# A delta-rule phase: convolution one iteration earlier, taps in PSUM, state product on a block-wise u

## The reference, cut to what matters

```python
q = silu(causal_conv4(x @ q_w, conv_q_w)); k = ...; v = ...       # depthwise, 4 taps
beta = sigmoid(x @ b_w)                                           # per token and head
q, k = l2norm(q), l2norm(k); v = v * beta; kb = k * beta
attn = where(strictly_lower, -(kb @ k.T), 0)                      # per chunk, 32 x 32
for i in range(1, 32):                                            # inverse of a unit triangle
    attn[i, :i] += attn[i, :] @ attn[:, :i]
attn = attn + eye; u = attn @ v; w = attn @ kb
for each chunk:                                                   # S is 32 x 32 per head
    u = u - w @ S
    o = q @ S + where(lower, q @ k.T, 0) @ u
    S = S + k.T @ u
o = g * o + (1 - g) * v                                           # g = sigmoid(x @ mix_w + ...)
out = (rms_norm(o) * o_norm_w) @ o_w
```

## Time and profile before

| what | us |
|---|---|
| median of 3 timed runs | 2016.2 (2015.22 to 2023.95) |
| the profiled execution: its span, and no other time of it is recorded | 2017.0 |
| delta phase in that trace, from about 1196 to 1812 | about 616 |
| busy share of the whole span: PE, DVE, ACT, POOL | 62%, 69%, 45%, 55% |

### The profile page before, as it was taken

One profiled execution on the slowest core, in us unless ns is written; L12 is line 12 of the kernel. 1 busy time (PEld: TensorE's weight loads), 2 busy tenths in 40 slices (PEclk: granted clock), 3 DMA queues, 4 the chain that ended last, 5 costly groups with the idle time before them and its releaser, 6 DMA issues. The chain is left out here.

```text
span 2017.0 us, 33672 instructions
## 1 busy us (share of the span) xinstructions
PE 1259.5 (62%) x13844; PEld 595.1 (30%) x13844; DVE 1388.5 (69%) x1689; ACT 915.8 (45%) x1673; POOL 1112.5 (55%) x479
## 2 busy tenths in 40 slices
PE   4464746556474756553488746577767767557875
PEld 1111212121221312120133323244444445443333
DVE  3799999999999999899650023776687668617002
ACT  5555564746556474644232214454455434123220
POOL 1889989899999989999600011322442344412000
PEclk9676768677676777775698877787778777668988
DMA  4827174472808356280299960112312222219997
GB/s 125 198 48 190 45 184 98 102 181 54 206 25 197 84 128 145 54 208 21 93 403 422 421 211 15 43 39 65 76 33 55 65 65 45 65 42 396 405 421 276
DMA packets 193705, 300.04 MB, mean 149 GB/s; under 512 B 82704, under 2 KB 125200, under 8 KB 177168
## 3 DMA queue, kind: packets, MB, share of 16 engines
q1 hardware_dynamic: 188512, 295.17, 48.5%
q10 hardware_dynamic: 4688, 2.19, 0.4%
q0 software_dynamic: 352, 0.52, 0.1%
HBM read 255.37 MB, written 42.47 MB: 148 GB/s over the span
## 5 line engine op out<-in xcount | busy, mean ns | idle before, releaser
L368 POOL TENSOR_TENSOR state<-dx_rep,b_rep 128x2048 f32<-128x2048 f32 x128 | 579.1, 4532 | 66.9 <-PE psum L736 35.7
L736 PE MATMUL psum<-state,sel 128*32 128x512 f32 x1024 | 193.6, 847 | 292.5 <-POOL state L377 292.5
L479 ACT ACTIVATE psum<-delta_rep,a_neg 128x511 f32<-128x511 f32 x512 | 331.5, 684 | 79.8 <-DVE state L598 79.7
L598 DVE TENSOR_TENSOR_SCAN psum<-psum,state 128x1024 f32<-128x1024 f32 x144 | 328.9, 2284 | 33.9 <-POOL state L368 24.0
L598 DVE TENSOR_TENSOR_SCAN state<-psum,state 128x1024 f32<-128x1024 f32 x112 | 255.2, 2279 | 19.9 <-ACT psum L479 19.9
L377 POOL TENSOR_TENSOR state<-state,c_rep 128x1024 f32<-128x1024 f32 x112 | 264.0, 2359 | 0.0
L667 PE MATMUL psum<-xt,w_in 128*128 128x512 f32 x256 | 161.0, 787 | 47.4 <-ACT z_silu L438 26.1
L605 DVE TENSOR_TENSOR state<-psum,c_rep 128x1024 f32<-128x1024 f32 x144 | 176.3, 1224 | 4.9
L736 PEld LDWEIGHTS psum<-state,sel 128*32 128x32 f32 x1024 | 27.5, 128 | 424.4 <-issue 391.4
L476 ACT COPY psum<-zeros 128x2 f32<-128x2 f32 x144 | 23.6, 164 | 257.9 <-DVE state L605 253.2
L1841 PE MATMUL psum<-xt_delta,w_qkv 128*128 128x512 f32 x192 | 111.4, 721 | 12.1 <-DVE attn_t L1655 11.3
(11 more groups left out here) (218 smaller groups left out, 2535.5 us busy)
## 6 DMA issues: line engine op xcount, KB each, us to landing
moe_w_set<-in_w SPq DMA_DIRECT2D x30, 4096.0 KB, 33.1
delta_rep<-delta_scratch SPq DMA_DIRECT2D x128, 256.0 KB, 5.4
dx_rep<-dx_scratch SPq DMA_DIRECT2D x128, 256.0 KB, 8.2
b_rep<-bc_scratch SPq DMA_DIRECT2D x32, 256.0 KB, 4.9
delta_scratch<-delta SPq DMA_DIRECT2D x32, 256.0 KB, 7.8
dx_scratch<-delta_x SPq DMA_DIRECT2D x32, 256.0 KB, 5.8
c_rep<-bc_scratch SPq DMA_DIRECT2D x32, 256.0 KB, 8.0
moe_x<-x_after SPq DMA_DIRECT2D x16, 512.0 KB, 8.5
```

The source lines that it names most:

```text
L368: nc.gpsimd.tensor_tensor(ring[q % RING][:, :, :], dx_rep[u % CHUNKS][:, :, :], free_bcast(b_rep[q // QPB % 2][:, g, :], 1, CB), ALU.mult) ...
L479: ins = nc.scalar.activation(dec[:, i, 1:], delta_rep[u % CHUNKS][:, c, 1:], ACT.Exp, scale=a_neg[:, dt * CB + c, g:g + 1])
L598: nc.vector.tensor_tensor_scan(bx if by_pool(k) else flat, flat, bx, 0.0, ALU.mult, ALU.add).then_inc(S["scan_done"], 1)
L736: ins = nc.tensor.matmul(bank[32 * c:32 * c + 32, :], sel[:, :], ring[q % RING][:, c, :], start=False, stop=(g == NG4 - 1), skip_group_che ...
```

## The change

1. The whole of a unit's convolution (six projects, last taps, taps) stands in its conv iteration, at slots 6 to 12, in two PSUM banks of its own (`cbank`). Last tap and taps work in place in the bank, and the third of VectorE's taps writes `conv_qkv`. A project from the third on waits for VectorE's last tap of the bank (`conv_done`) instead of ScalarE's read.
2. The front starts with silu at slot 0 (q, k) and slot 1 (v); one table set is loaded back, after v. Tokens are turned at slots 1 and 2, statistics at slot 4 (their rows now in 96 partitions), gram at slots 7 and 9, masks at 8 and 10.
3. SP sends x's residual, the next x, the n pair, the t pair, the output store.
4. `u_blk` has 128 partitions by 4 batches by 256 with zeros off its diagonal blocks. ScalarE writes u in four copies, and `k_times_u` is 8 matmuls over all 128 partitions in place of 32 small ones; the state is in one bank.
5. Outputs use one bank (`tbank`): `turn_outputs` at slots 6 and 7, `project_outputs` at 8 and 10, output adds at 9 and 11, each waiting for the one before.
6. POOL takes the carry of the convolution first and its second `solve_below` after the lambda mask. VectorE's solve rows are spread over slots 0 to 5, its products below stand at 6 and 9, and the gates at 7.

```diff
-    u_bank, o_bank, fbank = banks[0], banks[1], banks[6:8]
-    s_bank = lambda p: banks[2 + p]
+    u_bank, o_bank, s_bank, cbank, fbank, tbank = banks[0], banks[1], banks[2], banks[3:5], banks[5:7], banks[7]
...
-                    nc.scalar.copy(xpad[:, t, :, KC - 1:], bank[:, :].rearrange("c (p l) -> c p l", p=NP))
-                    nc.scalar.activation(raw[:, t, :, :], bank[:, :].rearrange("c (p l) -> c p l", p=NP), ACT.Copy,
-                                         scale=conv_w[:, t, KC - 1:KC]).then_inc(S["qkv_read"], 1)
+                    nc.scalar.copy(xpad[:, t, :, KC - 1:], bank)
+                    nc.scalar.activation(bank, bank, ACT.Copy, scale=conv_w[:, t, KC - 1:KC]).then_inc(S["qkv_read"], 1)
...
-                                nc.scalar.activation(u[:, :], u_bank[:, 0:D], ACT.Copy,
-                                                     scale=-1.0 if k % SPG else 1.0).then_inc(S["u_ready"], 1)
+                                for p in range(NP):
+                                    rows = slice(p * C, (p + 1) * C)
+                                    ins = nc.scalar.activation(u_blk[rows, p, :], u_bank[rows, 0:D], ACT.Copy,
+                                                               scale=-1.0 if k % SPG else 1.0)
+                                ins.then_inc(S["u_ready"], 1)
...
-                            nc.vector.scalar_tensor_tensor(raw[:, t, :, :], xpad[:, t, :, k:k + P], conv_w[:, t, k:k + 1],
-                                                           raw[:, t, :, :], ALU.mult, ALU.add).then_inc(
+                            if k == KC - 2 and w:
+                                dve.wait_ge(S["qk_feat"], w)
+                                dve.wait_ge(S["v_feat"], w)
+                            nc.vector.scalar_tensor_tensor(bank if k < KC - 2 else raw[:, t, :, :], xpad[:, t, :, k:k + P],
+                                                           conv_w[:, t, k:k + 1], bank, ALU.mult, ALU.add).then_inc(
...
-                            for p in range(NP):
-                                ins = nc.tensor.matmul(s_bank(p)[g * DK:(g + 1) * DK, hh * DK:(hh + 1) * DK],
-                                                       toks[w % COPIES][batch_rows(p), n, hc], u[batch_rows(p), hc],
-                                                       start=(k % SPG == 0 and hh == 0), stop=True, skip_group_check=True)
+                            ins = nc.tensor.matmul(s_bank[g * DK:(g + 1) * DK, hh * P:(hh + 1) * P],
+                                                   toks[w % COPIES][:, n, hc], u_blk[:, :, hc],
+                                                   start=(k % SPG == 0 and hh == 0), stop=True, skip_group_check=True)
...
-                        pe.wait_ge(S["qkv_read"], NT * w + j - 1)
+                        pe.wait_ge(S["conv_done"], NT * w + j - 1)
...
-                            if m < 5:
-                                project(f, m + 1)
+                            if m in (1, 2):
+                                for n in (0, 1) if m == 1 else (2, 3):
+                                    to_tokens(f, n)
...
+                        if conv is not None and 6 <= m < 6 + NT:
+                            project(a, m - 6)
+                        if front is not None and m in (7, 9):
+                            gram(f, (m - 7) // 2)
```

More of the change, by code:

```diff
@@ L1301, in state_blocks @@
             rows = slice(g * DK, (g + 1) * DK)
[L1302 removed]
+            return (s_bank[rows, 0:KD * P].rearrange("r (h p e) -> r p h e", h=KD, p=NP), state[rows, :, :, rows])
         def iterations(iteration):
@@ L1346, in iteration @@
                                 S[f"t_loaded{solve % 2}"], 16)
-                    if front is not None:
-                        sp.wait_ge(S["n_read"], HS * (front + 1))
+                    if tail is not None:
+                        sp.wait_ge(S["out_added"], 2 * (tail + 1))
                         for p in range(NP):
[L1350 to L1360, removed]
+                            sp.dma_start(unit_rows(x_out, tail, p), x_res[32 * p:32 * p + 32, :, :]).then_inc(
+                                S["x_stored"], 16)
                 iterations(iteration)
@@ L1374, in _ @@
                 nc.gpsimd.memset(eps_l2[:, :], 1e-12).then_inc(S["masks"], 1)
+                nc.gpsimd.memset(u_blk[:, :, :], 0.0).then_inc(S["masks"], 1)
                 for t_lane in t_lanes:
@@ L1441, in iteration @@
                                                 ALU.mult).then_inc(S["lam_mask"], 1)
[L1442 to L1447, removed]
-                        else:
-                            nc.gpsimd.memset(edge, 0.0).then_inc(S["carry"], 1)
+                    if solve is not None:
+                        solve_below(solve, 1)
                     if front is not None:
@@ L1680, in iteration @@
                             read_o(CT * tail + CT - 1)
-                        if solve is not None and m == 0:
-                            for row in range(1, 6):
-                                solve_row(solve, row)
-                        if front is not None and m == 1:
-                            taps(f, (0, 1))
-                        if front is not None and m == 3:
-                            taps(f, (2, 3))
-                        if conv is not None and m == 3:
+                        if conv is not None and m == 0:
                             dve.wait_ge(S["x_loaded"], 64 * (a + 1))
@@ L1694, in iteration @@
                                 nc.vector.bn_aggr(mv[:, n_, :], bn[:, n_, :]).then_inc(S["ln_mv"], 1)
+                        if solve is not None and m < 6 and m != 3:
+                            first, last = ((1, 6), (6, 9), (9, 12), None, (12, 14), (14, HC))[m]
+                            for row in range(first, last):
+                                solve_row(solve, row)
+                            if m == 5:
+                                copy_second(solve)
                         if tail is not None and m == 3:
@@ L1698, in iteration @@
                                                     ALU.add).then_inc(S["o_ms"], 1)
-                        if solve is not None and m in (4, 5):
-                            for row in (range(6, 9) if m == 4 else range(9, 12)):
-                                solve_row(solve, row)
-                        if conv is not None and m == 5:
+                        if conv is not None and m == 3:
                             dve.wait_ge(S["ln_rstd"], a + 1)
@@ L1705, in iteration @@
                                                            ALU.mult).then_inc(S["ln_shift"], 1)
[L1706 to L1718 removed]
+                        if front == 0 and m == 4:
                             dve.wait_ge(S["gates_loaded"], 16 * 4)
```

311 lines of the change are left out of this document (158 added, 153 removed).

## The result

The changed kernel takes 2024.5 us in the median (20 runs) against 2019.0 for the kernel before in the same runs: a ratio of 1.0021, 95% interval 1.0011 to 1.0031. That is slower by a trace, and within the 0.5% that I had called no change; forecast were 2020 us, and 1968 to 2054.

The account below looks back on a forecast made before the run. No engine was full; a loop of waits bounded the delta phase. Full iterations 0 and ramps +4.5 on 2017.0 gave about 2021, less 0.8 to the median 2020 us; range 1968 to 2054.

Parts of the forecast that it names:

- The n_lane wait is covered: VectorE before solve row 1: other work now fills the 7.34 us wait for n_lane, which goes.
- The t path: SP's t store and load now follow n; the first t_times_y of a unit ends 18.0 us after Z.
- rival C: Delta loop: late t path and conv_done wait idle TensorE, low clock follows; 73 us a loop, 2048 us; chance 0.27.
- Z: Delta phase: the time a unit's n_scratch store leaves SP, as its last mask ends; Z to Z is the loop's period.
- The loop, 66.6 to 68.4: Full delta iterations: serial sum 66.6 us, 68.4 with one low-clock project; middle 67.5 against 67.9 before, counted as 0.
- the marks behind t_times_y: Loop sum after t_times_y: turned rows copied at Z + 35.7, first conv bank free at Z + 50.4.
- Taps in PSUM: VectorE's conv taps: 680 ns each as in SBUF, so nil; by the skill page up to 9 us more.
- my sign of being wrong: VectorE's conv: taps of 740 ns and more in PSUM would show the prediction wrong.
- The state product: Each chunk: four u copies cost +1.1 us, k_times_u gains 0.1; fewer records save 0 to 1, taken as 0.
- Ramps: Delta phase outside full iterations: first Z +15, to second -7.5, last without conv -11, end +8; together +4.5 us.
- the forecast of no change: Whole kernel within 2006 to 2026 us, chance 0.26; same-length loop had 0.40, a tenth below, three tenths above.
- B: Rival for the delta loop: VectorE becomes the bound, 59 us a loop, 1980 us in all; chance 0.33.

Follow-up runs that it names:

- e2: The changed kernel with taps in SBUF again, a bank being free at ScalarE's read: 2022.9 us, ratio 1.0005 against the kernel before.
- e3: The changed kernel with SP's t pair ahead of the n pair and taps in SBUF: 1975.6 us, ratio 0.9766 against the kernel before.
- e11: The changed kernel with t pair first, projects spread, masks ahead of taps and all taps in SBUF: 1972.9 us, ratio 0.9758 against the kernel before.
- e9: The kernel before with u_blk and its four u copies alone, k_times_u still 32 small matmuls in four banks: 2030.7 us, ratio 1.0051.
- e1: The changed kernel with SP sending the t pair ahead of the n pair again: 2005.6 us, ratio 0.9917 against the kernel before.
- e4: The kernel before with the state product alone (u_blk, four copies, wide k_times_u, one state bank): 2014.8 us, ratio 0.9965.
- e8: The changed kernel with t pair first, projects spread over more slots, masks ahead of taps, taps in PSUM: 1983.9 us, ratio 0.9811 against the kernel before.
- e5: The changed kernel with t pair first, taps in SBUF and VectorE's masks ahead of taps: 1964.9 us, ratio 0.9723 against the kernel before.

## Why the prediction was right, and where it was not

*The n_lane wait is covered*: right. The 7.34 us of the earlier trace rows are gone. VectorE's waits for n_lane in the whole phase, before and after:

```profile
DVE prod L1625 <- DMA n_lane<-n_scratch: 65.1, 8, 9.1
```

```profile
DVE prod L1639 <- DMA n_lane<-n_scratch: 0.5, 1, 0.5
```

*The t path*: 18.0 forecast to the end of the first t_times_y, measured 1467.88 + 0.75 - 1450.48 = 18.2. Its lateness costs TensorE what rival C had named: the work ahead of it in the queue ran out at 1465.1, 14.6 us after Z.

*The loop, 66.6 to 68.4*: 67.6 measured, and the marks behind t_times_y held: in the iteration from 1450.48 the turned rows were copied at Z + 35.6, forecast 35.7, and the first bank was free at Z + 48.0, forecast 50.4. The step that failed is the one that takes the 18.0 us from Z as the only way to t_times_y. Projects 4 and 5 of the conv, the second half of the outputs and a chunk of the chain stand between Z and t_times_y on TensorE too; they wait for taps, and run beside the t path for 14.6 us. e2 and e3 show that both have to go. That the t path was the longer of the two, by 2.8 us there, let the sum come out, and nothing in the sum says so: that much of it was luck. I had one stretch at the low clock; two rows of about 3.78 an iteration are there.

*Taps in PSUM*: 751 and 742 ns against 745 ns of before, so a nil was right, though my reading was not. The 680 ns were a fifth of a row of five taps that overlap, and the output add's 686 beside it the length of one instruction; one tap alone took 745 before. So my sign of being wrong, taps of 740 ns and more, came up with nothing wrong. The estimate of 65 ns a tap, worked out from the Trainium skill, VectorE: DVE Perf Modes, section on the TRN2 errata, appears nowhere in these lengths. What I missed is the other side. In these traces VectorE is slower beside GpSimd where it reads two tensors from SBUF: beside the GpSimd rows of e3 six taps took 1.8 us each in the mean, and taps out of PSUM were not slowed beside those of the changed kernel. The Trainium skill has this in GPSIMD Engine Reference, section Specifications: the two engines share their SBUF interfaces, with contention for VectorE instructions that have two SBUF inputs. The rows of e3, e11 and the changed kernel agree with it.

*The state product*: the copies were sized rightly, 1.48 forecast for four and 1.52 measured:

```profile
1459.64 1.52 ACT L1505 ACTIVATE u_chunk<-psum 32x256 f32<-32x256 f32 x4
```

For them I put +8 us in the end and twice 1.1 in the loop, and 0 for fewer records. With the copies alone (e9) the loop is 1.8 us longer, the end 1.6, and the whole 10; the wide matmuls with the one bank return 17, about 0.5 us a chunk. The range of 0 to 1 us a chunk held it; I took the wrong end, 0.

*Ramps*, forecast and measured (the table's two first lines): to the first Z +15 and +17.4; to the second -7.5 and -9.1; second to third 0 and -2.8; full ones 0 and -1.2 together; the last without conv, seventh to eighth in the table and called sixth to seventh in the prediction, -11 and -7.8; the end +8 and +9.7. The sum is +4.5 and +6.2 us. The end came out by luck: e1 takes 5.9 of it away, so the late t path, which my sum had not there, has most of it, and e4 shows that the state product, which the sum had, has 1.8. The +15 was mainly the hand-off of the banks: without it the first Z comes 14.1 us sooner (e2 against the changed kernel), and 15.4 sooner with the projects spread (e11 against e8).

So the forecast of no change was right as a sum of gains and losses of up to 17 us each, and I had given that outcome a chance of 0.26 only; three tenths of 0.40 are 0.12 and not the 0.10 that I added, which would leave 0.24. The range's upper end, 2054, has no working behind it. The rivals: B's loop of 59 us is about what the kernel does without the two branches (e3 61, e5 60). Of C, the idling of TensorE at both places and the slow projects behind the taps were there; its price was not, as no loop of 73 was seen.

## What to carry to other kernels

Where a wait goes and the time stays, look for a branch that runs beside it: remove both, and only then judge the edit. A transfer's place in a program that runs in order is part of the change: here it cost 21 us, more than the 17 that the rest gained (e1). Where GpSimd works at the same time, see whether one of VectorE's two tensors can stay in PSUM, and set against it what the bank's longer use costs: in these runs it paid in the full loops and not before the first Z.

## What the runs showed of the hardware

An SBUF tap of 0.745 us took up to 2.4 us (e11), and six in a row 10.95 instead of 4.07 (e3), while GpSimd ran; taps out of PSUM stayed at 0.74 to 0.76. The shortest solve row is slowed too: in the changed kernel, beside GpSimd's product at 1465.91, it took 1.83 us instead of 0.16, and both ended at 1467.8:

```profile
1466.01 1.83 DVE L1639 TENSOR_TENSOR prod<-t_lane,n_lane 128x2 f32<-128x2 f32 x1
```

Wide matmuls, one in place of four small ones, made their own row little shorter (0.65 against 0.72 us). With them the idle time at the instruction behind, 19.8 us over the phase before and 11.4 with the copies alone (e9), was 0.5 us (e4).
